# Ending the first block with its expert loop, and interleaving the second block's opening batch by batch

## What is computed

```python
x = x + mamba_block(layernorm(x))       # selective scan, then a ReLU feed-forward 128-512-128
x = x + experts(layernorm(x))           # first expert layer
x = x + attention_block(layernorm(x))   # 16 heads of 8, rotary, causal, then a GELU feed-forward
x = x + experts(layernorm(x))           # second expert layer, same weights

def experts(x):                         # 24 experts, each token goes to its best 2
    gates = softmax(top2(x @ gate_w + gate_b))
    return x + sum(gates[k] * (gelu(x @ w1[e_k] + b1[e_k]) @ w2[e_k] + b2[e_k]) for k in (0, 1))
```

## Time and profile before

| | |
|---|---|
| three runs, us | 900.69, 905.30, 905.83 (median 905.3) |
| the profiled execution, us | 903.06, of which the span from first to last instruction 901.2 |
| busy, us of the span | PE 673.1, DVE 527.1, ACT 427.4, POOL 373.4 |
| mean granted TensorE clock | 0.87 of 2.4 GHz |
| the two stretches of 56 slot tiles, from PE's first to last transpose | 293.68 to 400.32 and 767.40 to 874.22 |

### The profile page before, as it was taken

One profiled execution on the slowest core, in us unless ns is written; L12 is line 12 of the kernel. 1 busy time (PEld: TensorE's weight loads), 2 busy tenths in 40 slices (PEclk: granted clock), 3 DMA queues, 4 the chain that ended last, 5 costly groups with the idle time before them and its releaser, 6 DMA issues.

```text
span 901.2 us, 19363 instructions
## 1 busy us (share of the span) xinstructions
PE 673.1 (75%) x5374; PEld 466.7 (52%) x5375; DVE 527.1 (58%) x1512; ACT 427.4 (47%) x908; POOL 373.4 (41%) x438
## 2 busy tenths in 40 slices
PE   2993888886930999990073999999996940999990
PEld 0430333333730999990041566556653730999990
DVE  6537999982552455546348777777712552455545
ACT  4225777756300555551444255665566310455560
POOL 6100999875276344454343021000005276254551
PEclk9996999997965899995587599999996965899995
DMA  7979999301011222213056311111001011222215
GB/s 218 327 221 241 246 251 247 85 9 62 7 41 49 76 69 67 68 45 100 7 152 180 105 37 54 38 35 35 20 9 64 7 41 48 75 69 68 68 46 149
DMA packets 89440, 84.15 MB, mean 93 GB/s; under 512 B 12448, under 2 KB 79640, under 8 KB 89112
## 3 DMA queue, kind: packets, MB, share of 16 engines
q1 hardware_dynamic: 83736, 71.73, 30.3%
q0 software_dynamic: 5632, 11.58, 3.9%
HBM read 37.95 MB, written 45.33 MB: 92 GB/s over the span
## 4 chain that ended last, share of the span: by engine, by line
PE 35%; POOL 4%; DVE 4%; issue 3%; ACT 2%; DMA 2%; SPq 0%; DVEq 0%; POOLq 0%; ACTq 0%
PE bank L636 6%; PE bank L645 6%; PE bank L1693 5%; PE bank L1632 3%; POOL xrows L372 3%; PE bank L1635 2%; PE bank L1669 2%; PE bank L1662 2%; PE bank L1666 2%; PE bank L1767 1%; PE bank L1704 1%; DVE X L550 1%; DVE t_ropes L1505 1%; PE bank L1775 1%; PE bank L629 1%
## 5 line engine op out<-in xcount | busy, mean ns | idle before, releaser
L1516 DVE TENSOR_REDUCE t_peak<-bank 128x1 f32<-128x512 f32 (+2 forms) x192 | 107.1, 597 | 37.3 <-PE bank L1635 36.4
L794 POOL TENSOR_TENSOR UN<-m_work 128x512 f32<-128x512 f32 x64 | 80.6, 1270 | 72.9 <-DVE m_work L974 72.9
L415 ACT ACTIVATE t_v_tiles<-bank,t_e_b1all 128x128 f32<-128x128 f32 x224 | 64.0, 368 | 61.9 <-PE bank L636 61.9
L415 ACT ACTIVATE m_dx_tiles<-bank,m_e_b1all 128x128 f32<-128x128 f32 x224 | 64.0, 369 | 61.8 <-PE bank L636 61.8
L380 POOL DMA_INDIRECT results<-m_XC,m_e_to_row x56 | 55.8, 996 | 65.2 <-DVE m_XC L535 62.7
L380 POOL DMA_INDIRECT results<-t_A,t_e_to_row x56 | 55.5, 991 | 65.6 <-DVE t_A L535 64.4
L974 DVE TENSOR_TENSOR_SCAN m_work<-bank,m_work 128x512 f32<-128x512 f32 x64 | 76.8, 1216 | 6.9 <-POOL UN L794 5.6
L1097 PE MATMUL bank<-UN,ident 128*128 128x512 f32 x128 | 70.0, 629 | 14.1 <-POOL UN L794 13.1
L525 DVE COPY UN<-w1all 128x512 f32 x112 | 48.0, 429 | 45.8 <-PE bank L636 37.2
L1352 POOL COPY t_tabs<-t_v_tiles 128x128 f32 (+1 forms) x16 | 4.7, 298 | 158.1 <-PE bank L1693 154.8
L636 PE MATMUL bank<-t_A,UN 128*128 128x128 f32 x448 | 61.3, 281 | 0.0
(11 more groups left out here) (332 smaller groups left out, 1540.3 us busy)
## 6 DMA issues: line engine op xcount, KB each, us to landing
xrows<-m_nothing SPq DMA_DIRECT2D x25, 1032.0 KB, 18.1
w1all<-in_e_w SPq DMA_DIRECT2D x6, 1024.0 KB, 12.2
m_dx_tiles<-xrows SPq DMA_DIRECT2D x56, 64.5 KB, 1.8
t_v_tiles<-xrows SPq DMA_DIRECT2D x56, 64.5 KB, 1.8
stacks<-t_front SPq DMA_DIRECT2D x24, 128.0 KB, 2.4
stacks<-t_hT SPq DMA_DIRECT2D x24, 128.0 KB, 2.4
t_tabs<-stacks SPq DMA_DIRECT2D x32, 96.0 KB, 2.2
t_hT<-stacks SPq DMA_DIRECT2D x32, 96.0 KB, 2.2
```

What stands on the lines that cost most here:

```text
L415: ins = act.activation(e.hid[:, mp, f * P:f * P + P], core.tiles(2 + mp)[:, f, :], ACT.Gelu, bias=row(e.b1all, x)[:, f:f + 1])
L794: g.tensor_tensor(hc[:, k % 4, :], h[:, k % 2, :], c_sb[:, k % 2, :], ALU.mult).then_inc(hc_ready, 1)
L1516: v.tensor_reduce(peak[p][:, qt, a, ss[0]:ss[-1] + 1], bank[:, ACROSS[a], 0:len(ss) * w].rearrange("p (j n) -> p j n", n=w), AX_X, ALU.max ...
```

## The change

- In both expert layers PE's list is written out for all 56 tiles: no hardware loop on PE. ACT and SP keep theirs.
- In both layers DVE makes the gate weights at tiles 28 and 29 and adds the residual tile by tile at tiles 8 to 23, inside its list for the slot tiles, instead of behind it.
- The first block ends with its slot tiles and with SP's start of the 8 reads of `results`. The read results and the gate weights now lie in tensors of both blocks (`core.work`, `core.gate`).
- Adding the results and the two norms (`combine`, `ln_0`, `ln_1`) move into the attention block, staggered with its opening: on DVE `join` (add and first statistics) and `again` (second statistics), on ACT the eight applications between the copies, on POOL the eight `norm_pool` between the cosine products, on PE each batch's transposes just before they are used.
- `keep` writes the parts with 3 DMAs for q and 3 for k of a batch instead of 6 and 6; the order of the rows in `stacks` changes to suit.
- `side` and `turnedqk` move to the memory of `A`, `hT` and two of the tiles `prob` to `core.work`.
- In both blocks the norm before the feed-forward is staggered: ACT copies the transpose of batch b-1 right behind the norm of b, the last one behind `bend(0)`; PE transposes batches 0 to 2, runs `hidden(0)`, transposes batch 3, and runs `hidden(1)`; each `hidden(b)` waits for its own copy.

The diff, cut to its core (what is left out passes tensors and semaphores about, and repeats the last point in the attention block):

```diff
+def combine(v, core, added, b, layer):
+    tiles = range(b * TT, b * TT + TT)
+    v.wait_ge(core.back_in[b], 16 * TOPK * layer)
+    for k in range(TOPK):
+        if k:
+            v.wait_ge(added[0], b * TT + TT)
+        for i in tiles:
+            v.scalar_tensor_tensor(out=core.X[:, i, :], in0=core.back[k][:, i, :], scalar=core.gate[:, k, i:i + 1],
+                                   in1=core.X[:, i, :], op0=ALU.mult, op1=ALU.add).then_inc(added[k], 1)
...
-        if e.layer == 1:
-            for b in range(NB):
-                norm_pool(g, core, e.ln_next, b)
-                if b >= 1:
-                    norm_pool(g, core, e.ln_1, b - 1)
-            norm_pool(g, core, e.ln_1, NB - 1)
...
-        v.wait_ge(e.gexp_ready, 1)
...
+            if j == GATES_AT:
+                v.wait_ge(e.gexp_ready, 1)
+                v.tensor_scalar(e.gsum[:], e.gexp[:], 1.0, None, ALU.add).then_inc(e.gate_step, 1)
+                v.wait_ge(e.gate_step, 1)
+                v.reciprocal(core.gate[:, 0, :], e.gsum[:]).then_inc(e.gate_step, 1)
+            if j == GATES_AT + 1:
+                v.wait_ge(e.gate_step, 2)
+                v.tensor_tensor(core.gate[:, 1, :], e.gexp[:], core.gate[:, 0, :], ALU.mult).then_inc(e.gate_step, 1)
+            if 0 <= j - SKIP_AT < NT:
+                v.tensor_tensor(X[:, j - SKIP_AT, :], X[:, j - SKIP_AT, :], XF[:, j - SKIP_AT, :], ALU.add)\
+                    .then_inc(e.skip_added, 1)
         v.wait_ge(e.gate_step, 3)
-        v.tensor_tensor(X[:], X[:], XF[:], ALU.add).then_inc(e.skip_added, 1)
-        v.wait_ge(e.skip_added, 1)
...
-        for b in range(NB):
-            v.wait_ge(e.back_in[b], 16 * TOPK)
-            for i in range(b * TT, b * TT + TT):
-                add(0, i, e.first_added)
-            v.wait_ge(e.first_added, b * TT + TT)
-            for i in range(b * TT, b * TT + TT):
-                add(1, i, e.second_added)
-            if layer == 1:
-                v.wait_ge(e.second_added, b * TT + TT)
-                norm_stats(v, e.ln_next, X, b)
-                if b >= 1:
-                    v.wait_ge(e.ln_next.normed, b * TT)
-                    norm_stats(v, e.ln_1, core.XN, b - 1)
-        if layer == 1:
-            v.wait_ge(e.ln_next.normed, NT)
-            norm_stats(v, e.ln_1, core.XN, NB - 1)
-            v.wait_ge(e.ln_1.normed, NT)
+        v.wait_ge(e.skip_added, NT)
+        if layer == 2:
+            for b in range(NB):
+                combine(v, core, e.added, b, layer)
...
-        def step(j, q, loop=False):
-            if e.has(j, 0, loop):
-                pe.wait_ge(core.slot_in[q], e.gathered + ((j - q) * (16 // AHEAD) if loop else (j // AHEAD) * 16) + 16)
+        def step(j, q):
+            if e.has(j, 0, False):
+                pe.wait_ge(core.slot_in[q], e.gathered + (j // AHEAD) * 16 + 16)
                 pe.wait_ge(e.xsT_ready, LEAD + j - 1)
                 pe.transpose(core.tiles(q % 2)[:, 0, :], e.xs[:, q, 0:D], core.ident[:]).then_inc(e.slot_turned, 1)
...
-        e.steps(pe, step)
+        for j in range(SLOT_TILES + 2):
+            step(j, j % AHEAD)
...
-            for b in range(NB):
-                norm_scalar(act, ln_2, XA, UN2, b)
-            for b in range(NB):
+            def turned_xa(b):
                 act.wait_ge(xa_turned, LEAD + b + 1)
                 act.activation(UT2[:, b, :], bank[:, b, :], ACT.Identity, bias=vec[:, LN2B:LN2B + 1],
                                scale=vec[:, LN2G:LN2G + 1]).then_inc(xaT_ready, 1)
             act.wait_ge(proj_ready, NB)
+            norm_scalar(act, ln_2, XA, UN2, 0)
+            for b in range(1, NB):
+                norm_scalar(act, ln_2, XA, UN2, b)
+                turned_xa(b - 1)
             def bend(b):
...
             bend(0)
+            turned_xa(NB - 1)
             bend(1)
...
-            for b in range(NB):
+            def turn_xa(b):
                 pe.wait_ge(ln_2.normed, b * TT + TT)
                 for t in range(TT):
                     tr = pe.transpose(core.tiles(b)[:, t, :], UN2[:, b * TT + t, :], core.ident[:])
                 tr.then_inc(xa_turned, 1)
-            pe.wait_ge(xaT_ready, LEAD + NB)
             def hidden(b):
+                pe.wait_ge(xaT_ready, LEAD + b + 1)
                 for f in range(FB):
+                    if b == 0:
+                        pe.wait_ge(xa_ready, f + 1)
                     pe.wait_ge(h1_relu, LEAD + FB * b + f - FB + 1)
                     pe.matmul(bank[:, 4 + f, :], w1[:, f * P:f * P + P], row(UT2, b),
                               start=True, stop=True).then_inc(h1_ready, 1)
...
+            for b in range(NB - 1):
+                turn_xa(b)
             hidden(0)
+            turn_xa(NB - 1)
             hidden(1)
...
-    Q_PARTS = (0, 0, 1, 0, 2, 1)
-    K_PARTS = (0, 1, 0, 2, 0, 1)
+    Q_PARTS = ((0, 0, 0), (1, 1), (2,))
+    K_PARTS = ((0, 1, 2), (0, 1), (0,))
...
+            placed = stacks.rearrange("x b h (d r) n -> x (b h d) r n", d=HD)
             def keep(b, p):
-                for x, pairs in ((0, Q_PARTS), (1, K_PARTS)):
+                for x, runs in ((0, Q_PARTS), (1, K_PARTS)):
                     sp.wait_ge(part_ready[x], b + 1)
-                    for r, i in enumerate(pairs):
-                        sp.dma_start(stacks[x, bass.ds(b, 1), :, r * HD:r * HD + HD, :].rearrange("a h d n -> (a h) d n"),
-                                     part[p][x][i]).then_inc(part_out[x][p], 16)
+                    r = 0
+                    for run in runs:
+                        n, i = len(run), 3 * x + run[0]
+                        src = parts[p][:, i:i + n, :] if run[0] < run[-1] else parts[p][:, i, :].unsqueeze(1).to_broadcast([P, n, T])
+                        sp.dma_start(placed[x, b * P:b * P + P, r:r + n, :], src).then_inc(part_out[x][p], 16)
+                        r += n
...
-            g.wait_ge(rope_in, 16 * 3)
-            for b in range(NB):
+            def times_cos(b):
                 g.wait_ge(qk_ready, LEAD + 2 * b + 2)
                 for x in range(2):
                     g.wait_ge(rope_ready, LEAD + 2 * b + x - 1)
                     g.tensor_tensor(side[:, x, :], qk[:, x, :], cos[:], ALU.mult).then_inc(cos_ready, 1)
+            norm_pool(g, core, ln_0, 0)
+            norm_pool(g, core, ln_0, 1)
+            norm_pool(g, core, ln_1, 0)
+            norm_pool(g, core, ln_0, 2)
+            norm_pool(g, core, ln_1, 1)
+            norm_pool(g, core, ln_0, 3)
+            g.wait_ge(rope_in, 16 * 3)
+            times_cos(0)
+            norm_pool(g, core, ln_1, 2)
+            times_cos(1)
+            norm_pool(g, core, ln_1, 3)
+            times_cos(2)
+            times_cos(3)
             g.wait_ge(va_set, 4)
...
+            norm_scalar(act, ln_0, X, XB, 0)
+            norm_scalar(act, ln_0, X, XB, 1)
+            norm_scalar(act, ln_1, XB, UN, 0)
+            norm_scalar(act, ln_0, X, XB, 2)
             act.wait_ge(qkv_in, 16 * 3)
-            for b in range(NB + 1):
...
+            keep_uT(0)
+            norm_scalar(act, ln_1, XB, UN, 1)
+            keep_qk(0)
+            norm_scalar(act, ln_0, X, XB, 3)
+            keep_uT(1)
+            norm_scalar(act, ln_1, XB, UN, 2)
+            keep_qk(1)
+            keep_parts(0)
+            norm_scalar(act, ln_1, XB, UN, 3)
+            keep_uT(2)
+            keep_qk(2)
+            keep_parts(1)
+            keep_uT(3)
+            keep_qk(3)
+            keep_parts(2)
+            keep_parts(3)
             act.preload_act_table(ACT.Exp)
...
-            v.wait_ge(qkv_in, 16 * 3)
-            v.wait_ge(rope_in, 16 * 3)
-            for b in range(NB):
+            def join(b):
+                combine(v, core, added, b, 1)
+                v.wait_ge(added[1], b * TT + TT)
+                norm_stats(v, ln_0, X, b)
+            def again(b):
+                v.wait_ge(ln_0.normed, b * TT + TT)
+                norm_stats(v, ln_1, XB, b)
+            def times_sin(b):
...
+            def take_apart(b):
...
+            join(0)
+            join(1)
+            again(0)
+            join(2)
+            again(1)
+            join(3)
+            again(2)
+            v.wait_ge(qkv_in, 16 * 3)
+            v.wait_ge(rope_in, 16 * 3)
+            times_sin(0)
+            again(3)
+            take_apart(0)
+            for b in range(1, NB):
+                times_sin(b)
+                take_apart(b)
...
-            for b in range(NB):
+            def turn_un(b):
+                pe.wait_ge(ln_1.normed, b * TT + TT)
...
                 tr.then_inc(un_turned, 1)
+            turn_un(0)
             for b in range(NB):
...
                 if b == 0:
                     pe.wait_ge(rope_in, 16 * 3)
+                if b < NB - 1:
+                    turn_un(b + 1)
                 for x in range(2):
                     pe.wait_ge(sin_ready, LEAD + 2 * b + x - 1)
                     pe.wait_ge(qk_ready, LEAD + 2 * b + x + 1)
```

118 lines of the change are left out of this document (55 added, 63 removed).

## The result

| | before | after |
|---|---|---|
| median of the runs | 904.6 us (900.7 to 905.8) | 881.2 us (878.9 to 883.8) |
| ratio, 95% interval | | 0.975 (0.971 to 0.979) |
| profiled execution, its span | 903.1 us, 901.2 us | 881.5 us, 879.6 us |

The kernel is 2.5% faster, 23 us by the medians and 21.6 by the two profiled spans. I had said 892, so 11.7 us of gain, with a range that ended at 884. The direction was right and the size was half of what came.

What follows compares the result with a forecast made beforehand. No one engine was taken to bound the kernel: PE paces the slot tiles, engine-to-engine chains the rest. Loop 4.0, norms 5.0 and boundary 2.7 sum to 11.7 us, from 903.1 to about 892, range 884 to 900.

Steps and rivals of the forecast that it cites:

- The meeting: End of first block: engines meeting and clearing semaphores cost 6.9 us, also after the change, behind SP's last read start.
- the boundary: Between the blocks: second block starts 24.75 us earlier, 22 go back, gain 2.7 us, bounds 0 and 7.
- The residual: End of DVE's slot-tile list: the 2.29 us addition was hidden, so removing it gives 0; its sixteen pieces cost 0.
- The norm before the feed-forward: Both blocks: copies slip between norms, so hidden(0) starts earlier; 2.5 us each, 5.0 in all, bounds 1.0 and 3.2 each.
- PE's loop: Slot tiles of both layers: removing the loop's edges of 0.45 us gains 2.0 a layer, 4.0 in all (0 to 5.2).
- Rival 1: Slot tiles: ACT's loop takes the place of PE's, the loops give 0, 895.4 us; chance 15%.
- The opening: Start of second block: engine lists followed from its start at 423.7, first peaks at 490.6 instead of 493.27.
- Rival 2: Opening of the second block: PE's clock stays low, the boundary gives 0, 894.1 us; chance 14%.
- keep: Second block: half as many DMA starts on SP, which the first peaks do not wait for; gain 0.
- gates: Slot tiles: gate weights made inside DVE's list, in steps where DVE idles; cost 0.
- moved buffers: Buffers placed in other memory: no instruction gets longer, 0.
- rival 3: More gain than said: opening's ACT waits close (7), loops 5.2, norms 3.0 each, 884.9 us; chance 13%.

Runs made afterwards that it cites:

- early drain: Kernel before with one more POOL drain straight behind the last scatter of each layer: 903.4 us, ratio 0.9960.
- drain between: Changed kernel with one more POOL drain in each layer, between the 32 scatters of routed rows and the 56 of results: 880.2 us, ratio 0.9712.
- last version: Changed kernel with POOL's opening list reordered and, in the first layer, one drain before the result scatters and four reads for eight: 871.3 us, ratio 0.9636.
- three other traces: Kernel before with the residual in 16 pieces, with it held back until all scatters landed, or with POOL drained early: 902.7, 901.7 and 903.4 us.
- one form of a kernel: Changed kernel with POOL's opening reordered; first layer: drains ahead of result scatters and behind every fourth, four reads for eight: 891.8 us, ratio 0.9857.

## Why the prediction fell short, step by step

- **The meeting, the step that failed most.** I took 6.9 us from ACT's last norm to the second block as a fixed price and put it behind SP's last read. The rows allowed another reading: ACT's end and the block's start are 6.9 apart, but nothing said that ACT was the last. It was POOL's drain, 7.3 us for 88 scatters: 5.6 of the 6.9 us were its part behind ACT's end, 1.3 the meeting. In after it runs beside SP's 5.3 us of starts. The block started 7.1 us behind the first read and not 12.1: 5.0 of the 5.3 us by which the boundary gave more. The early drain, the drain between and the last version show it in their traces (5.5, 0.6 and 2.7 us); in time the first gave 3.6.
- **The residual, "hidden, so 0".** It ended at 409.4, before SP's start at 411.6, and I stopped there. The row that I should have used is its neighbour: a last scatter of 2.98 us where the others took 0.96. What hides an instruction can be what it slows down. Worth 2.0 and 1.7 us.
- **The norm before the feed-forward: right in its mechanism, under-sized.** 2.5 each, measured 3.3 and 3.4 between the two kernels and 5.5 in time for both when undone. I let the copies of 0.69 us push the norms back. But in the old order the norms follow each other at 2.0 us, with 0.3 to 0.4 of waiting for POOL in between, and most of the first copy goes into that: the third norm stands 4.05 us behind the first without it and 4.18 with it. I had put it 4.4 behind, and hidden(0) at 7.2 where it stands at 6.8. The 0.6 to 1.1 us for the fourth transpose were not paid either: from hidden(0) to the first product behind it 8.5 us after, 8.7 before.
- **PE's loop.** 2.0 a layer, measured 1.3 and 2.2 between the two kernels, 2.3 a layer by the edges. The first is low since the clock rose one tile later there (an interval of 3.67 instead of 2.80). The row of 0.45 us an edge was the right price. The price of a compare-and-branch that I quoted from the Trainium skill (Advanced Engine Details and Errata, Control Flow Timing) isn't that of such an edge here. Rival 1 (ACT's loop takes over) fell: no edge is left in the intervals.
- **The opening.** 22 of the early start were to be given back; the lists, followed, came out within 0.5 us at the four landmarks, in part by luck. The 44.8 us of opening that the forecast measured them against are those of a first product at the full clock, which none of the three other traces has. The granted clock was 0.50 and 0.78 in the two parts of the stretch, 0.68 together, where I had said near 0.7; PE was at half clock for batches 0 and 2, behind 3.1 and 6.5 us of idling, and at full clock for batch 1. Rival 2 happened in part, and its cost was in the walk already.
- **keep, gates, moved buffers, the pieces of the residual:** 0. For keep a run shows it; the pieces of 0.28 us and the gates lengthen no step (1.90 us at most), DVE's wait ahead of its first copy shrinks from 0.39 to 0.23 us beside a piece. The moved buffers were not tried by themselves.
- **The range.** It ended at 884.9, since rival 3 was built from the bounds of terms that I had. Two terms were held at a value without a bound: the meeting at 6.9 and the residual at 0. With 0 to 5.7 for the meeting (the part behind ACT's end that has no work in it) and 0 to 2.0 a layer for the stretch of the scatter, both in rows that I had before me, it would have reached below 880.

## What to carry to other kernels

When engines meet, look for the one whose last instruction is a drain that goes on, not for the one whose last work is visible; work that is still to be started belongs beside it. An instruction that is hidden under another engine's must be compared with that engine's other instructions of the kind: if the neighbour is longer than its siblings, taking the hidden one away is not free of effect. And a price that is held fixed in a sum needs a bound from both sides as much as one that varies.

## What the runs showed of the hardware that I had not expected

- A drain of POOL ends 2.7, 4.6 and 7.3 us behind its last instruction after 32, 56 and 88 indirect scatters of 128 rows since the last drain: 0.082 us for each, also when the last of them was 30 us back. It isn't proportional down to small numbers: behind four scatters it still took 1.5 us (2.64 from its start, of which the last scatter has 1.2). A drain with no scatter since the one before it took 0.30.
- A scatter on POOL beside an addition of DVE with two inputs of 128x2048 gets on by 0.12 us in 1.4 and in 2.1 us: 0.96 us alone, 2.28 and 2.98 beside it.
- The edge of a loop on PE costs 0.44 to 0.58 us, with straight code of 34 instructions a step on either side costing nothing that can be seen (1.89 and 1.90 us a step).
- With the same code, the first product of the kernel before's second block ran at the full granted clock in one trace (behind 1.8 us of idling) and at half in three (behind 1.5 to 2.4 us). With the full clock went a first peak 44.8 us into the block, with half 47.9 to 48.3. So one trace is not enough to price such a stretch.
- Several engines can stand still together, with slot tiles 1.5 to 2.5 us longer, in one form of a kernel (by the times, 890.8 to 892.8, in all four of its runs), and not in another that differs in parts that run later. The cause is open.
